# A vision tower on one core: the front end two groups ahead, two cell tables, stem in two row tiles, loop written out

## The reference

```python
h = conv2d(x, stem_w, stem_b, stride 4)            # 96 channels, 24 x 24
h = leaky_relu(batchnorm(h, bn1))
offset = conv2d(h, off_w, off_b, stride 4)         # 32 values for each of 6 x 6 tokens
h = deform_conv(h, offset, dcn_w, dcn_b)           # 16 taps, each a bilinear sample of 4 corners
h = leaky_relu(batchnorm(h, bn2))                  # 192 channels, 36 tokens
t = tokens(h)                                      # then layer norm
h = t + layernorm(linear_attention(layernorm(t)))  # 12 heads, exp features
out = h + gated_expert_mlp(layernorm(h))           # 3 experts; the gate goes by the mean over an image
```

## Time and profile before

| | |
|---|---|
| median of 3 runs | 617.58 us |
| lowest, highest | 615.32, 622.56 us |
| span of the profiled execution | 614.2 us |
| PE / DVE / ACT / POOL busy in it | 474.5 / 316.3 / 225.9 / 182.8 us |
| mean granted TensorE clock | 0.872 of full speed |
| chain that ended last, by engine | PE 49%, DVE 20%, issue 9%, POOL 7%, DMA 6%, ACT 5% |

### The profile page before, as it was taken

One profiled execution on the slowest core, in us unless ns is written; L12 is line 12 of the kernel. 1 busy time (PEld: TensorE's weight loads), 2 busy tenths in 40 slices (PEclk: granted clock), 3 DMA queues, 4 the chain that ended last, 5 costly groups with the idle time before them and its releaser, 6 DMA issues.

```text
span 614.2 us, 8457 instructions
## 1 busy us (share of the span) xinstructions
PE 474.5 (77%) x2631; PEld 353.8 (58%) x2631; DVE 316.3 (51%) x1190; ACT 225.9 (37%) x537; POOL 182.8 (30%) x161
## 2 busy tenths in 40 slices
PE   3786063396982959989987949989889498799897
PEld 2463042164671757646875737656767375587786
DVE  2152244615646795185376962366489641537331
ACT  1513163302252553072653541353546430164321
POOL 2103478300135584000355771000368700000000
PEclk9977565597995798999998769999999799599999
DMA  3778453349964233008835330038652510000000
GB/s 69 151 204 235 155 154 107 106 109 276 272 221 129 78 92 92 1 1 229 262 120 145 92 109 24 1 83 243 193 154 72 145 31 0 0 1 1 15 1 14
DMA packets 58327, 67.37 MB, mean 110 GB/s; under 512 B 8158, under 2 KB 50470, under 8 KB 58290
## 3 DMA queue, kind: packets, MB, share of 16 engines
q1 hardware_dynamic: 47826, 38.54, 23.1%
q0 software_dynamic: 9216, 28.32, 15.7%
q10 hardware_dynamic: 1247, 0.07, 0.1%
HBM read 38.57 MB, written 28.35 MB: 109 GB/s over the span
## 4 chain that ended last, share of the span: by engine, by line
PE 49%; DVE 20%; issue 9%; POOL 7%; DMA 6%; ACT 5%; SPq 1%; ACTq 0%; POOLq 0%; DVEq 0%
PE bank L521 11%; POOL ring L391 7%; PE bank L673 7%; DVE acc L1049 6%; PE bank L662 5%; PE bank L430 4%; DMA cells<-ring 3%; PE bank L445 3%; DMA ring<-cells,cell 3%; PE bank L591 3%; PE bank L610 3%; PE bank L553 2%; PE bank L452 2%; PE bank L595 2%; ACT h L788 2%
## 5 line engine op out<-in xcount | busy, mean ns | idle before, releaser
L391 POOL DMA_INDIRECT ring<-cells,cell x144 | 170.5, 1184 | 273.3 <-DMA cells<-ring 192.5
L1049 DVE SCALAR_TENSOR_TENSOR acc<-ring,corner,acc 128x96 f32<-128x96 f32 x432 | 104.9, 317 | 62.2 <-ACT acc L805 61.8
L662 PE MATMUL bank<-xfT,w_up 96*128 96x288 f32 x288 | 87.1, 452 | 20.5 <-ACT hid L913 20.5
L673 PE MATMUL bank<-w_down,hid 128*108 128x192 f32 (+1 forms) x432 | 77.0, 332 | 5.4 <-ACT hid L913 5.4
L662 PEld LDWEIGHTS bank<-xfT,w_up 96*128 96x128 f32 x288 | 58.5, 213 | 36.2 <-ACT hid L913 21.4
L673 PEld LDWEIGHTS bank<-w_down,hid 128*108 128x108 f32 (+1 forms) x432 | 67.2, 165 | 11.9 <-issue 4.5
L805 ACT ACTIVATE acc<-ring,corner 128x96 f32<-128x96 f32 x144 | 42.6, 365 | 64.3 <-DMA ring<-cells,cell 64.3
L521 PE MATMUL bank<-shared,w_dcn 96*96 96x288 f32 x256 | 65.4, 417 | 0.6 <-issue 0.6
L430 PE MATMUL bank<-xt,w_stem 96*96 96x384 f32 x96 | 43.5, 591 | 22.1 <-ACT h L788 21.4
L521 PEld LDWEIGHTS bank<-shared,w_dcn 96*96 96x96 f32 x256 | 42.7, 168 | 21.6 <-issue 2.8
L913 ACT ACTIVATE hid<-bank,b_up 128x288 f32<-128x288 f32 x72 | 34.8, 497 | 45.2 <-PE bank L662 45.1
(11 more groups left out here) (144 smaller groups left out, 590.9 us busy)
## 6 DMA issues: line engine op xcount, KB each, us to landing
cells<-ring SPq DMA_DIRECT2D x16, 1656.0 KB, 18.3
xs<-in_x_dram SPq DMA_DIRECT2D x32, 108.0 KB
ring<-cells,cell POOLq DMA_INDIRECT x144, 3.2
w_up<-in_L_ffn_W_dram SPq DMA_DIRECT2D x2, 864.0 KB
w_down<-in_L_ffn_W_dram SPq DMA_DIRECT2D x3, 576.0 KB
hid<-in_L_tok_dcn_w_dram SPq DMA_DIRECT2D x1, 1152.0 KB, 11.5
out_dram<-y SPq DMA_DIRECT2D x8, 81.0 KB
w_qk<-in_L_attn_W_qkv_dram SPq DMA_DIRECT2D x24, 24.0 KB
```

The costliest lines, as they stand in the source:

```text
L391: pool.indirect_dma_start(ring[:, k % SLOTS, j, :], None, table[0:HALF_CELLS, :] if k < EARLY else table, bass.IndirectOffsetOnAxis(ap=cel ...
L662: mm = pe.matmul(ps[5 + n % 2][:, 0:TOK], w_up[:, kt, e, 128 * f:128 * f + 128], xfT[:, kt, :], start=(kt == 0), stop=(kt == 1))
L673: mm = pe.matmul(ps[DOWN_BANKS[e][t]][0:n, 0:C2], hid[:, e % 2, f, t0:t0 + n], w_down[:, e, f, :], start=(f == 0), stop=(f == FCH - 1))
L1049: ins = dve.scalar_tensor_tensor(dst, ring[:, k % SLOTS, j, C1 * c:C1 * (c + 1)], corner[:, BATCH * k + j, c // 2, c % 2:c % 2 + 1], dst, ...
```

## The change

- `ht` gets a buffer of its own, and there are two tables, two sets of `cell` and two of `corner`. `h` moves into `shared`, beside `samp`, `kp` and `qp` in turn.
- The prologue does the whole front end of groups 0 and 1; step g does that of group g+2, so only steps 0 and 1 have one.
- The stem works on two row tiles: a column of pixels takes 64 rows of `xt` (48 pixels, a row of ones, padding). Two products with 49 rows each, at row 0 and row 64, replace two products with 96 rows. Batch norm is folded into `w_stem`, so ACT copies without scale or bias.
- The offsets of a group are one pass of 16 products of 288 columns, where they were two passes of 16 with 144.
- `EARLY` is 5. The four-step loop is written out on each engine.
- In SP's order, the edges of both tables and the weights up to `w_up` come ahead of the images of group 1 and of `store_cells(0)`; `w_down` and `b_down` come behind `store_cells(1)`, which waits for the gathers of group 0.
- POOL does `rearrange_rows(g+1)` ahead of `gather(g)`.

```diff
-        def steps(eng, step):
-            step(0, False, True)
-            with eng.Fori(1, GROUPS - 1) as g:
-                step(g, True, True)
-            step(GROUPS - 1, True, False)
+        def steps(step):
+            for g in range(GROUPS):
+                step(g, g > 0, g + 1 < GROUPS, g + 2 < GROUPS)
...
             def store_cells(g):
-                if later(g):
+                if g >= 2:
                     for i in range(SLOTS):
-                        sp.wait_ge(gathered[i], 96 * g)
+                        sp.wait_ge(gathered[i], 96 * (g - 1))
...
             for kt in range(2):
                 sp.dma_start(w_up[:, kt, :, :], ...).then_inc(ld_ffn, 16)
+            load_images(1)
+            store_cells(0)
+            load_images(2)
+
+            for i in range(SLOTS):
+                sp.wait_ge(gathered[i], 96)
+            store_cells(1)
             for e in range(EXPERTS):
                 sp.dma_start(w_down[:, e, :, :], ...).then_inc(ld_ffn, 16)
...
+            def stem_channels(g, s, j):
+                u = 3 * s + j
+                pe.wait_ge(xt_evac, 6 * g + u + 1)
+                if u >= 1:
+                    pe.wait_ge(ch_evac, 12 * g + 2 * u)
+                for x in range(2):
+                    mm = pe.matmul(ps[2 + x][0:C1, 0:4 * ROWS], w_stem[TAPX * x:TAPX * x + KX + 1, :],
+                                   xt[TAPX * x:TAPX * x + KX + 1, 4 * j:4 * j + 4, :], start=True, stop=True)
+                mm.then_inc(ch_mm, 1)
...
+            def prepare_rest(g):                     # PE
+                stem_channels(g, 0, 1)
+                stem_x(g, 1, 0, 1)
+                stem_rows(g, 0, 0)
+                stem_channels(g, 0, 2)
+                stem_x(g, 1, 1, 2)
+                stem_rows(g, 0, 1)
+                stem_x(g, 1, 2, 3)
+                stem_channels(g, 1, 0)
+                stem_rows(g, 0, 2)
+                stem_channels(g, 1, 1)
+                stem_rows(g, 1, 0)
+                stem_channels(g, 1, 2)
+                stem_rows(g, 1, 1)
+                stem_rows(g, 1, 2)
...
+            def stem_ht(g, s, j):                    # ACT; DVE has the same wait
+                if later(g) and j == 0:
+                    act.wait_ge(h_stored[s], 32 * g)
+                act.wait_ge(ht_mm, 12 * g + 6 * s + 2 * j + 1)
+                act.activation(ht[:, s, 8 * j:8 * j + 4, :], ps[0][0:ROWS, 0:4 * C1], ACT.Copy).then_inc(ht_even, 1)
...
+            prepare(0)                               # ACT, prologue
             act.wait_ge(zeroed, 5)
             act.wait_ge(feat_ready, 1)
-            stem_bn(1, 0)
-            stem_xt(1)
+            prepare(1)
             combine_start(0)
-            stem_bn(1, 1)
...
             stem_xt(1)                               # DVE, prologue
+            leaky(1, 0, 0)
+            prepare_rest(1)
+            part_copy(1)
+            sample_points(1)
             combine(0, 0, 2)
...
                 norm_in(g)                           # DVE, step
-                if has_last and has_next:
-                    leaky(g + 1, 0)
-                    for j in range(3):
-                        leaky(g + 1, 1, j, j + 1)
-                        stem_ht(g + 1, 0, 2 * j + 1, 2 * j + 2)
-                if has_next:
-                    stem_ht(g + 1, 1)
-                    part_copy(g + 1)
-                    sample_points(g + 1)
+                if has_prep:
+                    prepare_rest(g + 2)
+                    part_copy(g + 2)
+                    sample_points(g + 2)
```

More of the change, by code:

```diff
@@ new lines, in offsets @@
+            def offsets(g):
+                pe.wait_ge(h_ready, 6 * (g + 1))
+                for kw in range(STRIDE):
+                    for kh in range(STRIDE):
+                        rhs = bass.AP(shared, kw * ROWS + kh,
+                                      [[TAPS * TOK, C1], [GRID * ROWS, 2], [STRIDE, SUB * OUT_SIDE], [STRIDE * ROWS, OUT_SIDE]])
+                        mm = pe.matmul(ps[4][32 * kh:32 * kh + 32, 0:TOK], w_off[:, STRIDE * kh + kw, :], rhs,
+                                       start=(kw == 0), stop=(kw == STRIDE - 1), skip_group_check=True)
+                mm.then_inc(off_mm, 1)
@@ L755, in step @@
                 up(g, 0, 1, 1)
-            steps(pe, step)
+            steps(step)
             g = GROUPS - 1
@@ L1250, in _ @@
             dve.wait_ge(zeroed, 5)
-            for s in range(2):
-                leaky(0, s)
-                stem_ht(0, s)
             part_copy(0)
```

401 lines of the change are left out of this document (197 added, 204 removed).

## The result

The changed kernel takes 643.25 us (median of 4 runs, 640.06 to 646.13), the kernel before on the same chip 620.07 (4 runs, 615.32 to 623.91): a ratio of 1.038, 95% interval 1.032 to 1.045. On another chip the same pair gave 638.26 and 620.13, ratio 1.038 (1.025 to 1.052). The profiled execution took 642.79 us, its span is 641.0, its mean granted clock 0.827 (0.872 before). The forecast was 620, the range reached to 632: both missed. Ratios here compare only the faster of the two levels that the executions of a kernel fall into, while medians take in all executions.

What follows compares the result with a forecast made beforehand. It took the path as prologue with first sampling, then steps, a whole front end costing 16 us in each. Terms 12.5 + 6 + 0.8 - 13.2 - 3.8 gave plus 2.3 on a 614.2 span, so 620 us; range 606 to 632.

Steps and rivals of the forecast that it cites:

- Prologue: Up to the first `w_dcn` products: later store of table 0 delays sampling, plus 12.5 us, bounds 6 and 18.
- The issue: SP queue in the prologue: store of table 0 starts at about 48 us, 12 later than before.
- The landing: Prologue: table 0's halves usable at about 68 and 82 us, after the distances of before, 19.6 and 34.6.
- The wait of `ht`: Prologue, `stem_ht`: group 1's copies wait for table 0's landing, 68 and 82 us; DVE combines from about 95.5.
- Front end in a step: Steps 0 and 1, new order and lower PE clock: plus 6 us (3 to 10) and plus 0.8 (minus 2 to 5).
- rival 1: Front ends of steps 0 and 1: PE stays at half clock, 11 us more, 631; chance 0.24 shared with long prologue.
- Stem and offsets: Front ends: row-tile pair 0.7 us if together, 1.3 if not; offsets save 2.2 us a group at full clock.
- rival 3: Stem: the row tiles run one after another, adding 5 us, 625; chance 0.06.
- Step 2: Step 2 loses its front end and becomes like step 3: minus 13.2 us (11 to 16).
- loop: Second iteration's start: writing the loop out removes DVE's idle gap, minus 3.8 us (0 to 5).
- rival 4: Loop: writing it out gives nothing, plus 3.8 us, 624; chance 0.45 together with the forecast.
- rival 5: Sampling phases: early gathers do pay, minus 11 us, 609; shares chance 0.25 with another rival that holds 0.17.

Runs made afterwards that it cites:

- e_sp2: Changed kernel with SP's weights `w_qk` to `w_up` issued behind `store_cells(0)`, a repeat of e_sp: 618.29 us, ratio 0.998 to the kernel before.
- e_ht_now: Changed kernel with group 1's `ht` in `w_up`'s space (`w_up` loaded later) and table 1's store straight behind table 0's: 622.81 us, ratio 1.002 to before.
- e_early: Changed kernel with `EARLY` = 2 instead of 5: one execution, 675.14 us, with standstills.
- e_best: Changed kernel, attention weights behind table 0's store, table 1's store at once, group 1's `ht` in `w_up`'s space, `EARLY` 2, 28 filling transposes: 615.73 us, ratio 0.9965.
- e_best2: e_best with DVE's front-end copies ahead of `norm_in` in place of the filling transposes: 608.31 us, ratio 0.979 to the kernel before.
- changed: The changed kernel itself, unaltered, run again in the second round: 638.26 us, ratio 1.038 to the kernel before.
- e_fill: Changed kernel with 28 unused transposes on PE where it waits for `norm_in` in steps 0 and 1: 633.30 us, ratio 1.029 to the kernel before.
- e_loop2: Kernel before with only its loop written out, a repeat of e_loop: 617.52 us, ratio 0.994 to the kernel before.
- e_sp: Changed kernel with SP's weights `w_qk` to `w_up` issued behind `store_cells(0)`, first round: 662.95 us, ratio 1.041 to before, with standstills.
- e_loop: Kernel before with only its loop of two iterations written out, first round: 631.50 us, ratio 0.993 to the kernel before.
- e_order: Changed kernel with DVE's front-end work (`leaky` and `ht` copies) ahead of `norm_in` in steps 0 and 1: 631.34 us, ratio 1.024 to before.
- e_ht1: Changed kernel with group 1's `ht` in the space of `w_up`, loaded later, so without the wait for table 0: 664.85 us, ratio 1.051 to before.

## Why the prediction was wrong

**Prologue: the mechanism right, the size off by 15.6 us.** This is the step that failed first: the term was plus 12.5 with an upper bound of 18, and it measured 28.1. It alone would have taken the forecast to 635.6, past the 632 of the range. By its own terms:

| term | predicted | after | off |
|---|---|---|---|
| store of table 0 issued | 48 | 54.2 | +6.2 |
| second half landed, from there | 34 | 40.9 | +6.9 |
| from there to `combine(0)` | 13.5 | 12.5 | -1.0 |
| from there to the first product | 38 | 41.4 | +3.4 |

(They sum to 15.5; the prediction had rounded 133.4 to 133.5.)

- *The issue.* The row copy came at 51.4, not at 45. SP came to the images at 36.7 and not 33.8, 2.9 us of it: the edges of two tables took it from 15.6 to 20.6 us where I had 3.3 us. The images then took 14.7 us and not 11.2: behind `w_up` they drained later than my sum of bytes by a rate. The bound from the rows was 56 and would have held; I cut it to 52 by judgement. e_sp2 and e_ht_now show what this queue is worth: without the weights, or without `w_up` alone, ahead of the images, the store is issued at 33.2 or 45.2, and e_sp2, which changes nothing else, is level with before.
- *The landing.* I took the 34.6 us of before. In the changed prologue it took 33.1 to 40.9, beside 15 gathers and not six; e_early, e_best and e_best2 stay between 32.7 and 34.4. Part of the term, about 3 us in the mean, is likely that contention; the rest of the 6.9 belongs to this execution (`changed` landed after 34.8 and lost 22 us in the prologue, not 28).
- *The wait of `ht`.* It did what the prediction said. From the landing to `combine(0)` it is 12.5 us in each of four executions with this prologue (107.58 less 95.09, 101.17 less 88.69, 98.91 less 86.40, 105.43 less 92.93), and also in e_sp2 (81.19 less 68.69). In e_ht_now, where the wait is gone, combining starts with the end of group 1's front end.
- *The end.* From `combine(0)` to the products it is 41.4 to 42.0 us in those four. I expected POOL's gather to be held for 5.9 us by DVE's burst, as in the earlier trace rows. It was held for 10.35 us, the burst having six batches at hand and lasting 12.46 us. So from batch 6 to the products it was 38.5 us (110.51 to 149.00) and not 35.5, which is nearly all of the 3.4. I had also misread: in the first sampling of before no batch from 6 on waits for DVE. POOL issues a gather each 1.25 us there, and its pace, with the one gather that is held, makes the 34.1 us.

**Front end in a step: the clock term and the price of the new order were both too small.** To `xn` I had 41.3 us in step 0 (37.0, 2.3 for the slow products, 2 for a lower clock) and 39.3 in step 1 (37.0 and 2.3); it measured 44.3 and 42.6, and 44.5 and 42.3 in the second profile. e_fill parts the terms. At full clock through the rows the same order took 40.6 and 38.4 us, 1.3 and 1.4 more than I had without the clock; the low clock cost 3.9 us in each step, where I had 2 and 2.3. With DVE's order turned round it was 35.6 in step 1, so my 37.0 lay between what the two orders can do.

The clock fell in both steps behind the wait for `norm_in`, as rival 1 said, and I had argued against it: in step 0 the L540 transposes of before took 0.71 us in spite of gaps around the same `norm_in`. But those come at the end of the stage. In the offsets just ahead of them (146 to 148 and 154 to 156 us) the granted clock of before is 0.50 as well:

```profile
146.00:148.00 2.00, 2.00 (x32) 1.35 (x26) 1.51 (x7) 0.00 (x0) 0.00 (x0) 0.50 1.11 326
154.00:156.00 2.00, 2.00 (x32) 1.33 (x32) 0.56 (x1) 0.00 (x0) 0.00 (x0) 0.50 1.05 329
```

The row that I read was not the row of the stage that I priced. Rival 1's own price, 7.6 us a step, was too high. The offsets take the same time at either clock (4.28 and 4.26 us), and the clock was back at 1.00 from 194 and from 329 us, right behind the first `xn` transposes, so the back end paid nothing for it.

**Stem and offsets.** The row tiles run together, so rival 3 is out: a pair takes 0.89 us at full clock, where six products of before took 4.75, 1.58 a pair (step 1 of before, granted clock 1.00 from 262 to 270 us):

```profile
268.19 4.75 PE L430 MATMUL bank<-xt,w_stem 96*96 96x384 f32 x12
```

I had 0.7 and 1.3, from a mean over the group. ACT's copies take 482 ns against 666, as expected. The offsets did not get cheaper: one group takes 4.27 us after and 2.30 + 2.26 us before, so 0.3 saved and not 2.2.

**Step 2** (minus 12.9 against 13.2) and the **loop** came as predicted. DVE's gap is gone, which is the row at 377.61 us, where the earlier trace rows had 3.83 us:

```profile
377.61 0.29 DVE L1221 COPY logit<-bank 108x3 f32<-108x3 f32 x3
```

The edit alone gave minus 4.3 and minus 3.9 us in two rounds (0.67% of 641.35, 0.63% of 621.04) against minus 3.8, both intervals below 1; rival 4 is out. That the gain is that gap is likely; the stages of e_loop2 do not show it.

**Early gathers** (rival 5) paid nothing that the stages show. In groups 1 to 3 the first six batches are in the ring long before DVE begins to combine, and the seventh waits for DVE for 51.4, 69.9 (at 373.03 us, group 2) and 59.1 us. The rows of before that the prediction read for this and did not show are these, POOL's timeline in step 0 and the group of `leaky`:

```profile
203.06 0.94 POOL L391 DMA_INDIRECT ring<-cells,cell  x1 [8.08 <-DVE acc L1049]
```

```profile
L1003 DVE SCALAR_TENSOR_TENSOR h<-h 96x768 f32<-96x768 f32 x24 | 21.5, 947 | 0.2
```

**The sum.** Plus 15.6 in the prologue, 5.5 in step 0, 2.9 in step 1, 0.3 in step 2 and 0.2 in the rest make 24.5, and with the 2.3 predicted the 26.8 us between the spans of 614.2 and 641.0. So the changed kernel is slower because its prologue went beyond its upper bound, with the front ends of steps 0 and 1 on top. Of the 8.4 us in these steps 3.0 and 3.3 lie ahead of `xn`; most of the rest lies behind `xn` in step 0, within the scatter there. The chances treated rival 1 and the long prologue as two ways to the same 624 to 640 us and did not add them.

**Where the gain of the idea went.** Two groups of lead took 13 us out of step 2, which has no front end any more, and writing the loop out gave 4. The price is a prologue in which two groups' front ends precede the first combining. With SP's order put right the balance is even (0.998), with group 1's `ht` elsewhere, two early batches and DVE's order turned round too it is 0.979 (e_best2).

**What stays open.** Why PE, DVE and ACT stood still for 3 to 21 us at a time without a releaser in the first round is not known. e_sp and e_sp2 are the same kernel, 662.95 us there and 618.29 here, e_loop and e_loop2 631.50 and 617.52, and the kernel before 641.35 and 621.04. So it goes with the chip or the hour, and it struck e_sp harder than e_loop. No run here shows its cause. In step 0, the way behind `xn`, 91.6 us after and 88.7 to 93.8 in the profiles of rounds 2 and 3 (88.9 before), was not taken apart either.

## What to carry to other kernels

When work is moved ahead of the first result, follow every DMA of the moved part through its queue: here the images of group 1 stood behind the weights, `w_up` with its 1.7 MB among them, that nobody needed before the end of step 0, and the order of that one queue was worth 4% of the time (e_sp2 0.998, the changed kernel 1.038 of before). When a buffer is written two groups ahead, ask which store must land before its next write, and what is queued behind that wait on each engine: here there were two tables, but one `ht`, and group 1's copies waited for the landing of table 0 all the same. Where PE must stop in front of a chain of small matmuls, read the granted clock in the same place of the trace of before and price the chain at 1.2 GHz too, or order the other engine's work so that PE need not stop.

## What the runs showed of the hardware

- A gap of 3.0 and 3.1 us on PE, behind work at full clock, was followed by a granted clock of 0.50 for the next 16 us (after, from 176 and from 310), one of 3.4 us by 0.50 for some 5 us (e_order, from 180 to 185). With 28 transposes in the gap the clock stayed at 1.00 through the rows (e_fill).
- The offsets, four column tiles of 32, take 4.26 us at a granted clock of 1.00 (e_order from 312.5 to 316.8) and 4.28 at 0.50 (after at 323.24). Transposes and stem products nearly double (0.82 to 1.51, 0.89 to 1.60). Something other than the clock sets the pace of these column tiles.
- A gather that POOL issued into DVE's first burst of combining was held for 10.34 or 10.35 us in nine profiles (after, changed, e_fill, e_order, e_sp, e_ht1, e_early, e_sp2, e_best2), where the burst was 54 instructions in 12.46 us. Shorter bursts held it shorter: 45 in 10.39 us for 9.32 (e_best), 36 in 8.36 us for 5.89 (before), 27 in 6.28 us for 4.51 (e_loop2). In the first sampling of e_ht_now, with no burst over 18, no gather took over 1.25 us.
- The store of table 0 (four DMAs of 1656 KB) had landed 33.1 to 40.9 us after its issue in four executions of the same prologue, and the first products moved with it, from 141.0 to 149.0 us.
